# Context features' products moved into the shared step as four stacked matmuls, and the last tower layers' hand-over taken apart by strips

## The reference, cut to what matters

```python
h = _ple_layer(e, W0, b0, G0w, G0b, Gs0w, Gs0b)   # 5 outputs of 1024
z = _ple_layer(h, W1, b1, G1w, G1b)               # 4 outputs of 1024
h = concatenate([z.reshape(1024, 4096), dense_ctx], axis=1)   # dense_ctx: 1024 x 16
h = maximum(h @ W_top1 + b_top1, 0)      # 4112 -> 512
h = maximum(h @ W_top2 + b_top2, 0)      # 512 -> 256
y = h @ W_top3                           # 256 -> 1
```

## Time and profile before

| | us |
|---|---|
| median of 3 runs | 2078.37 (2077.94 to 2079.14) |
| the profiled execution | 2094.69 |
| its span, first to last instruction | 2092.6 |
| TensorE busy | 2037.4 (97%), 8848 matmuls |
| VectorE busy | 1383.5 (66%) |
| ScalarE busy | 718.3 (34%) |
| GpSimd busy | 154.6 (7%) |
| granted clock of TensorE, mean | 0.989 |

### The profile page before, as it was taken

The page is one execution under the profiler, slowest core; times in us unless marked ns, Lnnn a source line. Parts: engine busy times, 40 slices in busy tenths (PEclk is TensorE's granted clock), DMA queues, the critical chain, the costliest instruction groups (busy, mean ns, idle before and its releaser), DMA issues.

```text
span 2092.6 us, 26712 instructions
## 1 busy us (share of the span) xinstructions
PE 2037.4 (97%) x8848; PEld 1654.4 (79%) x8848; DVE 1383.5 (66%) x1535; ACT 718.3 (34%) x966; POOL 154.6 (7%) x152
## 2 busy tenths in 40 slices
PE   7899999999999999999998999999999999999999
PEld 6778787788878888888776787877888788888887
DVE  4469788887256765656654698888862567566564
ACT  3233332333333333333432433333333332433333
POOL 5610000000000000000456000000000000000000
PEclk9999999999999999999998999999999999999999
DMA  6543333243233333233454333232332333233331
GB/s 207 157 135 101 114 97 119 82 131 93 80 118 94 111 93 118 91 112 101 133 167 136 119 101 121 90 121 91 120 100 73 121 95 114 93 111 94 117 91 41
DMA packets 70129, 230.23 MB, mean 110 GB/s; under 512 B 12494, under 2 KB 12814, under 8 KB 70076
## 3 DMA queue, kind: packets, MB, share of 16 engines
q1 hardware_dynamic: 61816, 208.55, 31.9%
q0 software_dynamic: 7488, 20.98, 3.2%
q10 hardware_dynamic: 772, 0.09, 0.0%
HBM read 229.36 MB, written 0.23 MB: 110 GB/s over the span
## 4 chain that ended last, share of the span: by engine, by line
PE 86%; DVE 5%; issue 4%; POOL 2%; ACT 1%; DMA 1%; another core or an unknown queue 0%; DVEq 0%; ACTq 0%; SPq 0%
PE main L309 25%; PE main L310 25%; PE main L311 25%; PE top L309 3%; PE top L310 3%; PE top L311 3%; POOL eo_b L300 2%; PE gps L344 1%; PE gps L346 1%; DVE w_lo L727 1%; DVE prod L798 1%; ACT w_hi L450 1%; DVE eo_b L798 1%; DVE act_lo L734 1%; DVE slots L871 1%
## 5 line engine op out<-in xcount | busy, mean ns | idle before, releaser
L309 PE MATMUL main<-act_hi,w_hi 128*128 128x512 f32 x2568 | 1008.7, 393 | 38.6 <-DVE w_lo L727 17.0
L310 PE MATMUL main<-act_lo,w_hi 128*128 128x512 f32 x2568 | 1005.6, 392 | 1.6 <-issue 1.5
L311 PE MATMUL main<-act_hi,w_lo 128*128 128x512 f32 x2568 | 1005.0, 391 | 0.7 <-issue 0.5
L450 ACT ACTIVATE w_hi<-raw 128x1024 fp32r<-128x1024 f32 (+1 forms) x360 | 380.5, 1057 | 1185.6 <-PE main L311 1032.6
L727 DVE TENSOR_TENSOR w_lo<-raw,w_hi 128x1024 fp32r<-128x1024 f32 (+1 forms) x360 | 438.6, 1218 | 513.8 <-ACT w_hi L450 471.0
L309 PEld LDWEIGHTS main<-act_hi,w_hi 128*128 128x128 f32 x2568 | 485.6, 189 | 161.6 <-issue 25.1
L311 PEld LDWEIGHTS main<-act_hi,w_lo 128*128 128x128 f32 x2568 | 485.6, 189 | 103.5 <-issue 1.4
L310 PEld LDWEIGHTS main<-act_lo,w_hi 128*128 128x128 f32 x2568 | 485.8, 189 | 101.4 <-issue 1.3
L804 DVE TENSOR_TENSOR slots<-slots,prod 128x1024 f32<-128x1024 f32 (+1 forms) x200 | 244.6, 1223 | 6.2 <-DVE prod L798 0.5
L300 POOL DMA_INDIRECT eo_b<-in_tbl,idx x144 | 150.5, 1045 | 992.8 <-DVE slots L804 889.7
L798 DVE TENSOR_TENSOR prod<-eo_sh,gate_b 128x1024 f32<-128x1024 f32 x136 | 165.7, 1218 | 3.8 <-DMA gate_b<-gates_dram 2.8
(11 more groups left out here) (69 smaller groups left out, 589.5 us busy)
## 6 DMA issues: line engine op xcount, KB each, us to landing
raw<-in_w SPq DMA_DIRECT2D x320, 512.0 KB
gate_b<-gates_dram SPq DMA_DIRECT2D x34, 512.0 KB, 4.5
raw<-in_w_top SPq DMA_DIRECT2D x32, 512.0 KB
gate_b<-gates_dram SPq DMA_DIRECT2D x16, 256.0 KB, 3.3
eo_b<-in_tbl,idx POOLq DMA_INDIRECT x144
raw<-in_w_top SPq DMA_DIRECT2D x4, 256.0 KB
gates_dram<-logit_t SPq DMA_DIRECT2D x18, 12.0 KB
gw_raw<-in_g_w SPq DMA_DIRECT2D x16, 16.0 KB
```

The source lines that it names most:

```text
L309: nc.tensor.matmul(dst, lhs_hi, rhs_hi, start=start, stop=False)
L310: nc.tensor.matmul(dst, lhs_hi, rhs_lo, start=False, stop=False)
L311: return nc.tensor.matmul(dst, lhs_lo, rhs_hi, start=False, stop=stop)
L450: nc.scalar.activation(w_hi[0:parts, slot, 0:cols], raw[0:parts, rawslot, 0:cols], ACT.Copy)\
```

## The change

**Context features.** There are no context units any more. The host lays the 16 weight rows and the 16 feature rows three times below each other, 48 partitions, one tensor `dense` for each half. SyncE loads it (192 KB) in the middle of the layer 1 shared step into `dense_raw`, a piece of `eo_b` that nothing uses in that step, after a new wait for the last layer 0 pair. ScalarE casts all 48 rows into `dense_k`; VectorE replaces rows 0 to 15 of the weights and rows 32 to 47 of the features by their low parts. One matmul over 48 rows is then the three products of `three` at once, and four matmuls, one for each bank, stand in unit 14 (`DENSE_HOST`) behind its fourth block. The passage to task 0's step becomes a plain `change`, whose list of gate operations on VectorE is empty. The ring's slot numbers of half 1 shift by two. In half 1 the matmuls wait for `y_rdy`, as the old ones did.

**The end.** The last tower units no longer go through `tower_slots` and `first_sums`. Bias and relu of bank m are placed right behind the split that follows its unit, the hand-over of strips 0 to 2 ahead of the end of the last unit, and strip 3 behind the split of the second half of `W_top2`, whose two splits now take 512 columns instead of 1024.

```diff
+STACK = 3 * DENSE
+DENSE_HOST = STEP - 2
...
+        dense_k = sb("dense_k", [STACK, TOP1 + N], f32r)
+        dense_raw = eo_b[0:STACK, 0:2, :].rearrange("p a n -> p (a n)")
...
-                stream(w1, 0, STEP, base + U_SH1, 0)
-                for d in range(2):
-                    slot = (U_DENSE + d) % RAW
-                    unit(w_dense, d, slot, base + U_DENSE + d, parts=DENSE, cols=TOP1 // 2)
-                    sp.dma_start(raw[0:DENSE, slot, TOP1 // 2:DENSE_COLS], dense_t[:, h * N:(h + 1) * N])\
-                        .then_inc(dctx_in[d], 16)
+                stream(w1, 0, STEP // 2, base + U_SH1, base % RAW)
+                sp.wait_ge(pair_done, p0 + 8 * (T + 1))
+                sp.dma_start(dense_raw, dense[h:h + 1, :, :].rearrange("a p n -> p (a n)")).then_inc(dense_in, 16)
+                stream(w1, STEP // 2, STEP // 2, base + U_SH1 + STEP // 2, base % RAW)
...
+            def dense_sums(h):
+                def emit(k):
+                    if k != 3:
+                        return
+                    if h:
+                        pe.wait_ge(y_rdy, h)
+                    pe.wait_ge(dense_rdy, 2 * (h + 1))
+                    for m in range(MT1):
+                        nc.tensor.matmul(top[m][:, :], dense_k[:, m * P:(m + 1) * P], dense_k[:, TOP1:TOP1 + N],
+                                         start=True, stop=False)
+                return emit
...
+                    if j == DENSE_HOST - 4 and dense_of is not None:
+                        act.wait_ge(dense_in, 16 * (dense_of + 1))
+                        nc.scalar.activation(dense_k[:, :], dense_raw, ACT.Copy).then_inc(dense_hi, 1)
...
-                act.wait_ge(dctx_in[0], 16 * (h + 1))
-                split_hi(0, 0, D0 // RAW, parts=DENSE, cols=DENSE_COLS)
-                evacuate(main[0][:, :], dest(STEP - 2), bias(STEP - 2))
-                hand_over(S + 1, 0, range(KT), D0)
...
+                change(U, V, off, dest, bias, S + 1, 0)
...
-            tower_slots(U, U // RAW, off, None, None, last=True)
-            first_sums(HALVES - 1)
-            S, U = s0 + HALF_STEPS, U + MT1
-            first_outputs(HALVES - 1, S, main + gps)
-            act.wait_ge(unit_done, U)
-            split_hi(1, (off + 1) % RAW, U // RAW + (off + 1) // RAW)
+            for m in range(MT1 - 1):
+                act.wait_ge(unit_done, U + m + 1)
+                if m < MT1 - 2:
+                    split_hi(m % 2, (U + m + 2) % RAW, (U + m + 2) // RAW)
+                else:
+                    split_hi(0, (U + MT1) % RAW, (U + MT1) // RAW, cols=2 * TOP2)
+                first_sum(m)
+            for k in range(MT1 - 1):
+                first_output(h, S, k)
+            act.wait_ge(unit_done, U + MT1)
+            split_hi(1, (U + MT1 + 1) % RAW, (U + MT1 + 1) // RAW, cols=2 * TOP2)
+            first_sum(MT1 - 1)
+            first_output(h, S, MT1 - 1)
...
+                    if j == DENSE_HOST - 3 and dense_of is not None:
+                        dve.wait_ge(dense_hi, dense_of + 1)
+                        for r, c in ((0, slice(0, TOP1)), (2 * DENSE, slice(TOP1, TOP1 + N))):
+                            part = slice(r, r + DENSE)
+                            nc.vector.tensor_tensor(dense_k[part, c], dense_raw[part, c], dense_k[part, c],
+                                                    ALU.subtract).then_inc(dense_rdy, 1)
...
+                change(U, V, off, S, 0, (None, lambda p: []))
```

More of the change, by code:

```diff
@@ L116, in build @@
         raw_in = [sem(f"raw_in{i}") for i in range(RAW)]
-        dctx_in = [sem(f"dctx_in{i}") for i in range(2)]
+        dense_in = sem("dense_in")
+        dense_hi = sem("dense_hi")
+        dense_rdy = sem("dense_rdy")
         gw_in = sem("gw_in")
@@ L478, in gate_slot, with step @@
                     nc.scalar.activation(lg[:, :, 0:rows_ // 2], lg[:, :, 0:rows_ // 2], ACT.Exp).then_inc(exp_rdy, 1)
-            def step(U, V, off, dest, bias, gates=None):
+            def step(U, V, off, dest, bias, gates=None, dense_of=None):
                 for j in range(1, STEP - 1):
@@ L642, in task0 @@
                     dest, bias = task_dest(t, S, Pb), biases(bias0, STEP + t * STEP)
-                    step(U, V, 0, dest, bias, (q0 + 1 + t, 2 * NG, 1 + t))
-                    change(U + STEP, V + STEP // RAW, 0, dest, bias, S + 1, (t + 1) * KT, shared=shared)
+                    step(U, V, off, dest, bias, (q0 + 1 + t, 2 * NG, 1 + t))
+                    change(U + STEP, V + STEP // RAW, off, dest, bias, S + 1, (t + 1) * KT, shared=shared)
                 with act.Fori(0, T - 1) as t:
@@ L876, in run, with step @@
                     op()
-            def step(U, V, off, ops=None, gates=None, split=None, plan=None, late=(), x=None):
+            def step(U, V, off, ops=None, gates=None, split=None, plan=None, late=(), x=None, dense_of=None):
                 sets = iter(range(NBT, ROWSETS))
@@ L938, in tower_slots, with first_outputs @@
                     split_lo(U + 5, 1, (off + 1) % RAW, V + 1 + (off + 1) // RAW)
-            def first_outputs(S):
-                for k in range(MT1):
+            def first_outputs(S, ks=range(MT1)):
+                for k in ks:
                     dve.wait_ge(act_hi_rdy, S * KT + 2 * (k + 1))
@@ L1001, in task0 @@
                                  h * 4 * T + t * 4)
-                    step(U, V, 0, ops, (q0 + 1 + t, NG, t * 2), (q0 + 2 + t, NG), plan)
-                    return change(U + STEP, V + STEP // RAW, 0, s0 + 2 + t, (t + 1) * KT, ops, shared=last)
+                    step(U, V, off, ops, (q0 + 1 + t, NG, t * 2), (q0 + 2 + t, NG), plan)
+                    return change(U + STEP, V + STEP // RAW, off, s0 + 2 + t, (t + 1) * KT, ops, shared=last)
                 with dve.Fori(0, T - 1) as t:
@@ L1011, in _ @@
                 U = u0 + U_SH1
[L1012 to L1013 removed]
+                step(U, U // RAW, off, late=left, dense_of=h)
+                U = u0 + U_T1
                 V, S = U // RAW, s0 + T + 2
[L1015 to L1021 removed]
+                change(U, V, off, S, 0, (None, lambda p: []))
                 E, Pb, Q = e0 + (T + 2) * STEP, p0 + 8 * (T + 1), q0 + T + 1
@@ L1045, in _ @@
                     tower_slots(U, U // RAW, off, steps(h + 1)[0], 4 * KT, x=h + 1)
-            tower_slots(U, U // RAW, off, None, None, last=True)
-            first_outputs(s0 + HALF_STEPS)
+            for m in range(MT1 - 2):
+                split_lo(U + m + 2, m % 2, (U + m + 2) % RAW, (U + m + 2) // RAW)
             U += MT1
-            split_lo(U + 1, 1, (off + 1) % RAW, (U + 1) // RAW)
+            split_lo(U, 0, U % RAW, U // RAW, cols=2 * TOP2)
+            first_outputs(s0 + HALF_STEPS, range(MT1 - 1))
+            split_lo(U + 1, 1, (U + 1) % RAW, U // RAW, cols=2 * TOP2)
+            first_outputs(s0 + HALF_STEPS, range(MT1 - 1, MT1))
 LINKS_L0 = 7 + 4 * 6 + 4 * 2
```

79 lines of the change are left out of this document (28 added, 51 removed).

## The result

| us | before | after |
|---|---|---|
| median, measured side by side | 2078.76 (2077.94 to 2080.56, 4 runs) | 2062.68 (2062.10 to 2065.56, 4 runs) |
| ratio | | 0.9924, interval 0.9907 to 0.9941 |
| the profiled execution | 2094.69 | 2062.24 |
| its span | 2092.6 | 2060.4 |
| granted clock of TensorE, mean | 0.989 | 0.998 |

The forecast was 2064.8. The change takes 16.1 us off the median, 13.6 were expected. The two profiled executions differ by 32.4 us, twice as much. The one of before, 2094.69, isn't among the runs of this comparison and lies 14 us above the slowest of its four; the one of after is among its four. Where the rest of the difference lies is the first thing to clear up.

What follows compares the result with a forecast made beforehand. TensorE's chain of matmul starts was taken to bound the kernel (86% of the chain). Old stages 13.6, less stacked matmuls 2.5, plus the end 2.5 gave 13.6 us off 2078.37: 2064.8 us, range 2062.0 to 2069.0.

Steps and rivals of the forecast that it cites:

- Term 1: Old context stages between shared step and next step: removing them saves 7.59 + 6.05 = 13.6 us, about 5 of it clock.
- the rival that the fall happens anyway: The clock still falls at or behind the old stage's place, so 5 us are not won: 2069.8 us; chance 0.09.
- C: Theory of the experiments, not the forecast: narrow matmuls together with the hole among them bring the lower clock level.
- The seam: Shared step into task 0's step of layer 1: no wait for new activations, cost 0; rival 1.7 us a half, chance 0.06.
- Term 2: Four stacked 48-row matmuls in unit 14 cost 1.25 us a half, 2.5 in all, range 1.8 to 3.9.
- The operands' preparation: Loading, casting and subtracting for the stacked matmuls on SyncE, ScalarE and VectorE: all hidden, cost 0.
- the rival on the slower side: ScalarE's wait for the new transfer stops TensorE and makes the kernel slower, for instance 2083 us; chance 0.03.
- Term 3: Last tower matmul to second tower layer's last: 5.44 instead of 8.18 us, saving 2.5 us, range 2.3 to 2.7.
- The sum and the base: Terms give 13.6 us, taken unscaled off the median of 2078.37: 2064.8 us.
- the step on the base: Profiled execution is 16.3 us, 0.8%, longer than the median; scaling 13.6 by that changes only 0.1, so terms stay unscaled.

Runs made afterwards that it cites:

- b_again: The kernel before, unchanged, run once more: 2098.34 us, ratio 1.0008 to the kernel before measured beside it.
- tripled: The changed kernel with eight more useless 48-row matmuls behind the four; executed once, read by stretches: 8.63 us between ScalarE's two splits over that unit.
- a_again: The changed kernel, unchanged, run once more with more rounds: 2087.31 us, ratio 0.9951 to the kernel before.
- padded_rows: The kernel before, context operands zero-padded from 16 to 128 rows, hole kept; run twice; 6.79 us from shared step's last matmul to the next step's 11th.

## Why the prediction was right, step by step

**Term 1, the old stage.** Right that the stage brings the fall of the clock and, on average, right in its size. The five us of clock were taken as a cost of the stage, against the rival that the fall happens anyway; stretches at 1.00 in all ten stages of the new form bear that out, and C says why. By the padded stages the clock's part is 2.2 us a half on average, 4.4 in all. The doubt about the two halves was in its place as well: which half has the long fall is chance (b_again), so the sum of both, 13.6, was better than twice either. Over the six old and eight new distances from shared step to tower (means 538.69 and 533.28) the net gain is 5.4 us a half, 10.8; the forecast had 13.6 - 2.5 = 11.1.

One reason given for this term is wrong, though the sum doesn't rest on it. The hole was put down to the first six narrow matmuls, which had to free buffer 1. The second context unit's rows of ScalarE and VectorE in before say otherwise:

```profile
584.74 0.83 ACT L450 ACTIVATE w_hi<-raw 16x768 fp32r<-16x768 f32 x1
...
585.70 0.95 DVE L727 TENSOR_TENSOR w_lo<-raw,w_hi 16x768 fp32r<-16x768 f32 x1
```

ScalarE began before the sixth of these matmuls had even started (585.35), and neither engine has idle time ahead. Buffer 1 is free once the shared step's last matmul (583.77) is done. What stood in the way was the hand-over queued before the split: ScalarE's eight casts (4.75 us from 580.08), then VectorE's eight subtractions (4.91 us from 580.73).

**The seam.** Right: 0.22 us. The empty queue of VectorE was the reason given; the earlier trace rows had shown it for the same code.

**Term 2.** 1.34 us a half by TensorE, 1.37 by ScalarE, 2.7 in all; 2.5 were forecast. The missing 0.1 a half is the second full matmul on the way out (0.34 us after the first, not 0.23). I had counted both matmuls on the way in and only the first on the way out. The weight loads stand beside the matmuls: those of half 1 begin at 1590.92, the matmuls at 1590.93. Row of the loads:

```profile
1590.92 0.76 PEld L375 LDWEIGHTS top<-dense_k 48*128 48x128 f32 x4 [0.35 <-issue]
```

The four loads take 0.76 us and the stacked matmuls keep the plain pace in tripled, so none of it is added. The Trainium skill, page "TensorE: Matmul & The Clock Gate", section "Part 3: Packing small matmuls — row/col tiling", lets a load overlap a running matmul only in another row group. By that rule the four would have cost near 2.0 us a half; all of these use the same first rows, and this case's trace doesn't agree. The same section elsewhere lets a load go ahead of running matmuls also into the background weight buffer, and with that sentence the trace agrees.

**The operands' preparation.** 0, as said, but not for each reason given. SyncE was to find its new wait already met; it stopped there for 4.2 us in both halves. The cost is 0 because the next load of weights wasn't allowed before then either. ScalarE's copy came at 545.93 (forecast near 551.6), the splits ended at 553.5 (near 560). The transfer took 2.9 us and lay 35 us ahead of its use; the rival on the slower side never came near.

**Term 3, the end.** 2.74 us, where 2.5 was taken and 2.74 named as the most that it could be. The slack of 1.1 us, worked out from the earlier trace rows, was 1.1 and 1.2. I had shaded the term for a lateness that the slack already excluded. That no fall of the clock can follow the old hole any more is an extra I hadn't seen; it was worth 1.3 us in two of seven traces, and none in the first pair.

**The sum and the base.** The touched stretches give 10.8 + 2.7 = 13.5 to 13.6 us, as forecast, and the mean of the three ratios says 13.5. The measured 16.1 lies 2.5 above, one of three comparisons that run from 9.8 to 16.1. If the rest of before's profiled execution (1631.5) is what it is in every run, a run of 2078.4 has heads of 446.9 us, and by the same working one of after has 445.3: less than 2 us of chance in favour of after. That is worked out from single traces, not shown.

What was weak is the step on the base. The 16.3 us between the profiled execution and the median were called 0.8% and treated as a scale over the whole kernel. They are no scale: the eight distances from shared step to tower of the new form in the table agree within 0.8 us, while the two heads together run from 445 (after) to 467 us (a_again) with the same code. The uncertainty of a comparison is that of the heads, and 2062.0 to 2069.0 held no term for it. With the 9.8 us of a_again the time would have been 2068.6, at the range's edge. The forecast in absolute us held because the median that it starts from, 2078.37, comes from the occasion of the result (2078.76 beside it); the same kernel took 2097.07 and 2100.55 on the others. Nothing in the working vouched for that; in this point the forecast was lucky.

## What to carry to other kernels

A narrow stage between two steps can cost much more than its matmuls: here 2.7 us of matmuls had 1.4 us of hole among them, and the lower clock that followed cost 1.7 or 3.2 us in each half. Where such a stage has to stay, zero rows up to 128 took the clock's part away. Otherwise give such matmuls operands that are ready long before and put them between full ones without a wait; whether inside a unit or at the seam made no difference here. Compare two executions by distances between fixed instructions around the edit, never by their totals, and look first at how far stretches differ that the edit doesn't touch.

## What the runs showed of the hardware that I had not expected

A stop of 1.4 to 1.7 us among narrow matmuls was followed by the lower clock level every time (8 of 8), one of 1.67 us among 128-row matmuls never (0 of 4), and one of 2.57 us with full matmuls on both sides in two of seven traces. How long the fall lasts (3.4 or 6.8 us at the old stage) varies between executions of the same code. Why the zero rows of padded_rows keep the clock up when the same numbers are computed isn't shown by anything here.

Padding by zeros costs nothing in matmul time: 16 rows have a pace of 0.23 us, 48 rows 0.229 (tripled), 128 rows 0.227. The other two engines look the same: ScalarE's copy of 48x1024 took 1.04 us, of 128x1024 1.06; VectorE's subtraction of 16x512 0.70 (1.39 for two), of 128x512 0.69.

The two heads, where VectorE transposes gathered rows, took 445 to 467 us together in three executions of the changed kernel. VectorE's waits for these gathers don't make the difference: in the second head of after, the shortest, they are 31.7 us in 15 waits, in that of before 8.3 us in 5. The granted clock does go with it, 0.99 and 0.98 in the two heads of after, 0.96 in both of a_again. What sets which occasion gets the short heads stays open. Of the separate question whether the products could also have stayed twelve, each with its own rows, nothing was tried.
